# A fused two-layer cross-attention and expert kernel: new written-out orders for all five engines, and separate statistics tiles for the second row norm

## The chip, the core and the metric

The kernel runs on one core of one Trainium2 chip. A core has five engines with an instruction queue each: TensorE (PE, matrix products), ScalarE (ACT), VectorE (DVE), GpSimd (POOL) and SyncE (SP, which here only issues DMAs). They run side by side and meet at semaphores. The metric is the device time of one execution, in microseconds (us); less is better.

## What is computed

32 sequences of 128 rows by 128 features go through four steps, each added to its input. The letters a, b and c are the kernel's names for its stages.

```python
x = x + _L0_xattn_ref(_layernorm(x), ctx_1024, ctx_1024, mask_BxS2_if1, ...)   # a: 16 heads of 8, causal, bf16
x = x + _L0_ffn_ref(_layernorm(x), Ws1, Ws2, W1, W2, Wr)                       # a: shared part and 8 experts
x = x + _L1_xattn_ref(_layernorm(x), ctx_1024, mask_Bx1xSxS2_ff0, ...)         # b: 16 heads of 8, with a bias
x = x + _L1_ffn_ref(_layernorm(x), q_w, k_w, v_w, o_w, sel_v_w, sel_o_w, rs)   # c: 8 heads of 128, gated experts
...
def _L1_ffn_ref(x, q_w, k_w, v_w, o_w, sel_v_w, sel_o_w, route_scale):
    gate_v = _get_sel_gate(x, sel_v_w, rs)      # sigmoid, the best 2 of 8 experts for each head
    gate_o = _get_sel_gate(x, sel_o_w, rs)
    q = jnp.einsum('bsd,hpd->bhsp', x, q_w.reshape(H, P, D))
    k = jnp.einsum('bsd,hpd->bhsp', x, k_w.reshape(H, P, D))
    xv = jnp.einsum('bsd,hedp->bshep', x, v_w.reshape(H, E, D, P))
    v = jnp.einsum('bshep,bshe->bhsp', xv, gate_v)
    att = jax.nn.softmax(jnp.einsum('bhqp,bhkp->bhqk', q, k) * SCALE, axis=-1)
    ctx = jnp.einsum('bhqk,bhkp->bqhp', att, v)
    weighted = ctx[:, :, :, None, :] * gate_o[..., None]
    return jnp.einsum('bshep,hepd->bsd', weighted, o_w.reshape(H, E, P, D))
```

The last step is most of the work: all 64 value experts and all 64 output experts are computed for every row and weighted by gates that are zero for six of eight.

## The kernel before

**Stages.** Each batch (one sequence) passes four stages in a software pipeline of about five batches in flight. The calls beginning with `a_` are the first layer: the norm of x (`a_stats`, `a_root`, `a_norm`), the transposed context, keys and queries (`a_ctxt`, `a_keys`, `a_queries`), the scores and their maxima (`a_scores`, `a_max`, `a_maxt`, `a_withmax`), the second norm of the first layer (`a_stats2`, `a_root2`, `a_norm2`), its transpose `a_x1t`, and the experts. The `b_` calls are the second attention (`b_scores`, `b_bias` with the row maxima nmB, `b_exp`, `b_trans`, `b_proj`). The `c_` calls are the third norm (`c_stats`, `c_norm`, which writes xnC), its transpose `c_xt`, the routing (`c_choice`, `c_gates`), and the attention among rows (`c_products`, `c_scores`, `c_max`, `c_exp`, `c_trans`, `c_context`). `values(b, h)` and `outputs(b, h)` are the value and output experts of head h; on PE a third argument is the half of four experts.

**The experts on five engines.** For each half of four experts PE makes three products into one half of the PSUM tile psC (`Vh`, `Vl` or `Oh`, `Ol` are the two parts into which each weight is split). ACT multiplies the four blocks of one half by their gates into TE, DVE multiplies the four of the other half and adds what ACT has written, and POOL adds them up (`accO` for the outputs, `v_sb` for the values). psC has two halves that PE uses in turn, whatever it writes; scores and transposes of the `c_` part take turns in it too. The turn is kept by the helper `pair`:

```python
            def pair(key):
                p = place[key] = turn[0] % 2
                turn[0] += 1
                return psC[:, p], emptied[p]
```

so each write to a half waits for whoever reads it last.

**What sets the order.** Nothing is scheduled when the program is built. Each engine has three written-out lists of calls: `start()` (the fill), `period(i)`, called for i from 7 to 31 and unrolled, and `end()` (the drain). An engine does its list strictly in order, and every call waits at the semaphores of what it needs. A name may stand in another list in the changed file only because the place where the period is cut has been moved; what counts is the row of calls that results. SP's list holds the DMAs: `inputs(b)` (x and context), `masks`, `bias`, `b_keys` (12 small copies that build the block keys bdB), `a_keys` and `a_queries` (four small copies each, bdA and Qb), `store(b)`, and at the start the weights; `products2` loads `k_w`, `products` loads `q_w`. The 16 calls `load` and `cut` bring in and split the expert weights, beside the first two batches; ACT issues the loads.

**Row norms.** `spread` makes a norm's statistics in three operations on DVE, with POOL's `root` and DVE's `normal` behind it. The first and the second norm of a batch share stA, mvA and rsA.

## Time and profile before

| | us |
|---|---|
| median of 3 runs | 1480.84 (1480.16 to 1483.44) |
| the profiled execution | 1481.03 |
| its span | 1479.2 |
| fill (to the first `a_max` of batch 6) | 257.87 |
| 25 periods (to the first `a_max` of batch 31) | 1078.31 |
| drain | 143.02 |

| engine | busy, share of the span | busy in one part of a period, 815.47 to 834.37 | busy in the other, to 858.58 |
|---|---|---|---|
| PE | 95% | 18.60 of 18.90 | 24.14 of 24.21 |
| DVE | 87% | 17.06 | 22.10 |
| ACT | 86% | 18.90 | 20.05 |
| POOL | 58% | 10.41 | 16.18 |

A row of a timeline tells when an instruction (or several alike, with their count) started, how long it ran, and in brackets how long its engine had been idle before it and what ended that wait. The mean granted clock of TensorE was 0.979 of full, and it was full through the loop.

### The profile page before, as it was taken

To read this page: it belongs to the slowest core of one execution; us is meant where nothing else is said; L and a number is where in the kernel's file an instruction comes from. 1 tells how busy PE (TensorE), PEld (TensorE's weight loads), DVE (VectorE), ACT (ScalarE), POOL (GpSimd) and SP (SyncE) were. 2 spreads that over 40 slices of the span, in tenths; PEclk is the share of its full clock that TensorE was granted. 3 is DMA by queue.
4 is the path that set the end of the run, shared out by engine and by line. 5 is a ranking of instruction groups with operands and counts; after the bars stand their busy time and mean duration, and the time that the engine had idled before them with its cause. 6 is when DMAs were issued, how large, how long until landed. Compare 5 with 4: busy or idle time off the path is not lost.

```text
span 1479.2 us, 34876 instructions
## 1 busy us (share of the span) xinstructions
PE 1404.5 (95%) x9748; PEld 963.9 (65%) x9905; DVE 1283.9 (87%) x5266; ACT 1275.8 (86%) x4428; POOL 859.0 (58%) x1345
## 2 busy tenths in 40 slices
PE   4678999999999999999999999999999999999998
PEld 2455666666676666667666666766666676666654
DVE  3677988998998999899899999989999998998886
ACT  3657888899988889998888999888899988889886
POOL 3113656556565656656565565656556565655567
PEclk8689999999999999999999999999999999999999
DMA  4410000000000000000000000000000000000000
GB/s 136 139 56 16 10 14 16 15 15 12 15 11 14 16 15 15 12 15 11 14 16 15 15 13 15 11 14 16 15 15 13 15 11 14 14 15 7 8 3 4
DMA packets 68960, 30.18 MB, mean 20 GB/s; under 512 B 19168, under 2 KB 68768, under 8 KB 68768
## 3 DMA queue, kind: packets, MB, share of 16 engines
q1 hardware_dynamic: 51552, 19.31, 4.9%
q10 hardware_dynamic: 17216, 8.65, 2.1%
q8 instruction: 79, 1.29, 0.4%
q14 instruction: 113, 0.93, 0.2%
HBM read 17.31 MB, written 2.10 MB: 13 GB/s over the span
## 4 chain that ended last, share of the span: by engine, by line
PE 62%; ACT 13%; DVE 11%; POOL 7%; issue 4%; SPq 2%; DMA 1%; POOLq 0%; ACTq 0%; another core or an unknown queue 0%; DVEq 0%
PE psC L309 43%; PE psA L309 7%; PE psB L309 6%; DVE nmA L2240 5%; ACT PTA L1344 3%; ACT PS L1344 3%; POOL accO L3405 3%; DVE PTB L2365 3%; ACT TE L1344 3%; DVE TE L2497 2%; ACT PTB L1344 2%; SPq L3776 2%; PE psA L421 1%; POOL accO L3413 1%; PE psB L553 1%
## 5 line engine op out<-in xcount | busy, mean ns | idle before, releaser
L3405 POOL TENSOR_TENSOR accO<-accO,TE 128x512 f32<-128x512 f32 x192 | 246.3, 1283 | 143.9 <-DVE TE L2497 137.7
L1344 ACT ACTIVATE TE<-psC,gate 128x128 f32<-128x128 f32 x1024 | 300.1, 406 | 17.7 <-PE psC L309 10.4
L1344 ACT ACTIVATE TE<-psC,gateO 128x128 f32<-128x128 f32 x1024 | 292.5, 375 | 24.8 <-PE psC L309 16.2
L2497 DVE SCALAR_TENSOR_TENSOR TE<-psC,gate,TE 128x128 f32<-128x128 f32 x1024 | 284.5, 339 | 29.5 <-PE psC L309 18.4
L2497 DVE SCALAR_TENSOR_TENSOR TE<-psC,gateO,TE 128x128 f32<-128x128 f32 x1024 | 287.1, 341 | 13.2 <-PE psC L309 8.2
L3393 POOL TENSOR_TENSOR TE<-TE 128x256 f32<-128x256 f32 x256 | 192.4, 752 | 164.5 <-DVE TE L2497 160.4
L309 PE MATMUL psC<-Vh,xTh 128*128 128x512 f32 x512 | 263.3, 514 | 2.3 <-ACT PS L1344 1.2
L309 PE MATMUL psC<-Oh,ch 128*128 128x512 f32 x512 | 262.9, 513 | 0.2
L309 PE MATMUL psC<-Oh,cl 128*128 128x512 f32 x512 | 203.0, 396 | 0.0
L309 PE MATMUL psC<-Vh,xTl 128*128 128x512 f32 x512 | 202.5, 396 | 0.0
L309 PE MATMUL psC<-Ol,cb 128*128 128x512 bf16 x452 | 176.2, 390 | 0.0
L1344 ACT ACTIVATE PTB<-PTB,nmB 128x128 f32<-128x128 f32 x512 | 167.2, 434 | 3.5 <-DVE nmB L2365 3.5
L309 PE MATMUL psC<-Vl,xTb 128*128 128x512 bf16 x419 | 163.5, 390 | 0.0
L309 PEld LDWEIGHTS psC<-Ol,cb 128*128 128x128 bf16 x512 | 49.0, 96 | 140.6 <-issue 140.6
L309 PEld LDWEIGHTS psC<-Vl,xTb 128*128 128x128 bf16 x512 | 49.2, 96 | 139.5 <-issue 139.5
L3398 POOL TENSOR_TENSOR v_sb<-TE 128x128 f32<-128x128 f32 x256 | 118.5, 463 | 17.6
L2365 DVE CUSTOM_DVE_ANT_0 PTB<-psB,bias_sb 128x128 f32<-128x128 f32 x512 | 114.5, 284 | 3.2 <-PE psB L309 3.2
L309 PEld LDWEIGHTS psC<-Vh,xTh 128*128 128x128 f32 x512 | 98.7, 193 | 28.3 <-ACT PS L1344 10.5
L2240 DVE TENSOR_REDUCE nmA<-psA 128x4 f32<-128x512 f32 x128 | 84.8, 684 | 34.5 <-PE psA L309 34.3
L309 PEld LDWEIGHTS psC<-Oh,ch 128*128 128x128 f32 x512 | 99.0, 193 | 9.8 <-DVE cl L2489 0.9
L1344 ACT ACTIVATE PTA<-psA 128x512 f32<-128x512 f32 x160 | 101.7, 675 | 2.3 <-PE psA L309 1.2
L309 PEld LDWEIGHTS psC<-Oh,cl 128*128 128x128 f32 x512 | 97.6, 191 | 6.2
(228 smaller groups left out, 3426.7 us busy)
## 6 DMA issues: line engine op xcount, KB each, us to landing
bdB<-Kc SPq DMA_DIRECT2D x384, 16.0 KB
raw<-in_L_ffn_v_w ACTq DMA_DIRECT2D x8, 512.0 KB, 4.5
raw<-in_L_ffn_o_w ACTq DMA_DIRECT2D x8, 512.0 KB, 4.2
x_sb<-in_x SPq DMA_DIRECT2D x32, 64.0 KB, 2.1
ctx_sb<-in_ctx SPq DMA_DIRECT2D x32, 64.0 KB, 2.0
bdA<-Kc SPq DMA_DIRECT2D x128, 8.0 KB
Qb<-Qc SPq DMA_DIRECT2D x128, 8.0 KB
bias_sb<-in_mask_Bx1xSxS_ff SPq DMA_DIRECT2D x32, 64.0 KB, 1.9
```

The lines of the kernel that those rows point to most:

```text
L309: return T.matmul(o, l, r, start=start, stop=stop)
L421: m = T.transpose(psA[:, 1, t * P:(t + 1) * P], UA[:, t * P:(t + 1) * P], ident)
L553: m = T.transpose(psB[:, 1, t * P:(t + 1) * P], Qh1f[:, t * P:(t + 1) * P], ident)
L1344: return A.activation(o, i, func, **kw)
L2240: V.tensor_reduce(nmA[:, t, :], heads_of(psA[:, t % 2, :]), AX_X, ALU.max, negate=True).then_inc(a_nm, 1)
L2365: m = V.tensor_tensor_reduce(PTB[:, t, j], psB[:, t % 2, j * P:(j + 1) * P], bias_sb[:, b % 2], -1.0, LEAST, ALU.add, ALU.min, nmB[:, t, j ...
L2497: m = V.scalar_tensor_tensor(TE[:, i, e], psC[:, p, e * P:(e + 1) * P], gates[:, e:e + 1], TE[:, i, e], ALU.mult, ALU.add)
L3393: G.tensor_tensor(TE[:, i, 0:2], TE[:, i, 0:2], TE[:, i, 2:4], ALU.add).then_inc(v_fe, 1)
L3398: G.tensor_tensor(v_sb[:, h], TE[:, i, 0], TE[:, i, 1], ALU.add).then_inc(v_fe, 1)
L3405: G.tensor_tensor(accO[:], TE[:, slot(b, H1)] if h == 1 else accO[:], TE[:, slot(b, H1 + h)], ALU.add).then_inc(o_fe, 1)
L3413: G.tensor_tensor(accO[:, 0:2], accO[:, 0:2], accO[:, 2:4], ALU.add).then_inc(o_fe, 1)
L3776: SY.dma_start(dst, src).then_inc(s, 16)
```

## The change

**Statistics.** The second norm of the first layer gets tiles of its own, stA2, mvA2 and rsA2. **Order.** The lists of all five engines are written anew. Over the 32 batches each engine makes the same calls as before (2,562 on PE, 1,943 on ACT, 2,809 on DVE, 1,347 on POOL, 265 on SP), in another order.

```diff
         rsA = sb("rsA", [P, 1])
+        stA2 = sb("stA2", [P, 6])
+        mvA2 = sb("mvA2", [P, 2])
+        rsA2 = sb("rsA2", [P, 1])
...
-                spread(x1[:], stA, mvA, rsA, a_ln2, b, n)
+                spread(x1[:], stA2, mvA2, rsA2, a_ln2, b, n)
...
-                normal(xnA, x1[:], mvA, rsA, a_ln2)
+                normal(xnA, x1[:], mvA2, rsA2, a_ln2)
...
-                root(rsA, a_rs2)
+                root(rsA2, a_rs2)
...
+                a_x1t(i - 1)
+                b_proj(i - 2)
                 outputs(i - 4, 0, 1)
-                a_x1t(i - 1)
```

The places of the loop's and the fill's lists that matter most follow.

PE in a period, about the scores. `psC<-Oh,ch` and its two neighbours are one half of `outputs(i - 5, 7)`, `psB<-bdB,Qs` is `b_scores`, `psA<-bdA,Qb` with the mask's product is one `a_scores`, and `psC<-ident_r,xnC` is `c_xt`. Before:

```order
L309 MATMUL psC<-Oh,ch 128x512
L309 MATMUL psC<-Oh,cl 128x512
L309 MATMUL psC<-Ol,cb 128x512
L309 MATMUL psB<-bdB,Qs 128x512 x2
L309 MATMUL psA<-bdA,Qb 128x512
L309 MATMUL psA<-late_b,ident_b 128x4x44
L575 MATMUL psC<-ident_r,xnC 128x128
L309 MATMUL psA<-bdA,Qb 128x512
L309 MATMUL psA<-late_b,ident_b 128x4x44
L629 MATMUL psC<-ident_r,PS 128x128 x4
```

Now:

```order
L312 MATMUL psC<-Oh,ch 128x512
L312 MATMUL psC<-Oh,cl 128x512
L312 MATMUL psC<-Ol,cb 128x512
L312 MATMUL psA<-bdA,Qb 128x512
L312 MATMUL psA<-late_b,ident_b 128x4x44
L312 MATMUL psA<-bdA,Qb 128x512
L312 MATMUL psA<-late_b,ident_b 128x4x44
L578 MATMUL psC<-ident_r,xnC 128x128
L312 MATMUL psB<-bdB,Qs 128x512 x2
L632 MATMUL psC<-ident_r,PS 128x128 x4
```

Both first `a_scores` have moved ahead of the last two `b_scores`, and `c_xt` stands behind them.

DVE at the same place. `TE<-psC,gateO,TE` is `outputs(i - 5, 6)`, `nmA<-psA` is `a_max`, and the rows with nmB are `b_bias`. Before:

```order
L2365 ISA nmB 128x1
L2365 ISA PTB,nmB<-psB,bias_sb 128x128
L2365 ISA nmB 128x1
L2497 SCALAR_TENSOR_TENSOR TE<-psC,gateO,TE 128x128 x4
L2240 TENSOR_REDUCE nmA<-psA 128x4
L2365 ISA PTB,nmB<-psB,bias_sb 128x128
L2365 ISA nmB 128x1
L2365 ISA PTB,nmB<-psB,bias_sb 128x128
```

Now:

```order
L2368 ISA PTB,nmB<-psB,bias_sb 128x128
L2368 ISA nmB 128x1
L2500 SCALAR_TENSOR_TENSOR TE<-psC,gateO,TE 128x128 x4
L2223 TENSOR_SCALAR xnC<-x,mvC,rsC 128x128
L2243 TENSOR_REDUCE nmA<-psA 128x4
L2368 ISA PTB,nmB<-psB,bias_sb 128x128
L2368 ISA nmB 128x1
L2368 ISA PTB,nmB<-psB,bias_sb 128x128
L2368 ISA nmB 128x1
```

The third norm's last step (`xnC`, `c_norm`) stood 31 rows further ahead, and now stands between the outputs and the first `a_max`.

SP at the start of the fill. `in_L_ffn_q_w` and `in_L_ffn_k_w` are the weights of `products` and `products2`, and `in_x` with `in_ctx` is `inputs`. Before, from the 14th issue:

```order
L3776 DMA Ws2s<-in_L_ffn_Ws 64x128
L3776 DMA W2s<-in_L_ffn_W 128x4x128
L3776 DMA raw<-in_L_ffn_sel_v_w 64x128
L3776 DMA raw<-in_L_ffn_sel_o_w 64x128
L3776 DMA rs<-in_L_ffn_route_scale 128x1
L3776 DMA raw<-in_L_ffn_q_w 128x8x128
L3776 DMA mrow_i<-in_mask_BxS_if 16x128
L3776 DMA raw<-in_L_ffn_k_w 128x8x128
L3776 DMA bdA<-Kc 8x4x128 x4
L3776 DMA bdA<-keyrow 1x16x128
L3776 DMA Qb<-Qc 8x4x128 x4
L3776 DMA x_sb<-in_x 128x128
```

Now, from the 8th:

```order
L3779 DMA Wv1s<-in_L_xattn_wv 128x128
L3779 DMA Wo1s<-in_L_xattn_wo 128x128
L3779 DMA x_sb<-in_x 128x128
L3779 DMA ctx_sb<-in_ctx 128x128
L3787 DMA bq_raw<-in_L_xattn_bq 128x1x1
L3779 DMA raw<-in_L_ffn_k_w 128x8x128
L3779 DMA mrow_i<-in_mask_BxS_if 16x128
L3783 DMA bk_raw<-in_L_xattn_bk 128x1x1
L3779 DMA raw<-in_L_ffn_q_w 128x8x128
L3779 DMA x_sb<-in_x 128x128
L3779 DMA ctx_sb<-in_ctx 128x128
L3779 DMA Qb<-Qc 8x4x128 x4
```

The two large weights have moved ahead of the experts' weights of the first layer, and the inputs of batch 1 ahead of the block queries and keys.

On DVE `a_stats(i, 0)` of the next batch has moved from behind the values to right behind `a_maxt`, and in the fill `a_stats(1, 0)` stands ahead of the operations that build the block queries and keys of batch 0. In the drain DVE's `c_choice(31, 4)` and `c_choice(31, 5)`, which stood around `c_products(31, 0)`, stand behind `c_max(31, 1)`. On ACT, `c_xt` stands behind the copies of the keys in the fill where it stood ahead of them, and in a period `a_values2` and `values(1)` stand behind the last `a_exp`. On SP `bias(3)` stands ahead of `b_keys(2)`, where it stood between `b_keys(2)` and `a_keys(3)`.

## Rows read from the trace of the kernel before

**Rows 1.** The page: busy time and share of the span; granted clock, 40 slices.

```profile
PE 1404.5 (95%) x9748; PEld 963.9 (65%) x9905; DVE 1283.9 (87%) x5266; ACT 1275.8 (86%) x4428; POOL 859.0 (58%) x1345
...
PEclk8689999999999999999999999999999999999999
```

**Rows 2.** Busy time by stretch: fill, loop, a period's parts, half clock, drain.

```profile
core 0: us, PE busy (x) PEld busy (x) DVE busy (x) ACT busy (x) POOL busy (x), PEclk, DMA share, GB/s
0.00:257.87 257.87, 204.07 (x1400) 140.62 (x1420) 189.25 (x755) 185.08 (x601) 102.22 (x193) 0.89 0.20 56
257.87:1336.18 1078.31, 1069.06 (x7602) 739.09 (x7726) 978.44 (x4076) 973.98 (x3426) 665.27 (x1027) 1.00 0.05 14
815.47:834.37 18.90, 18.60 (x174) 13.24 (x175) 17.06 (x74) 18.90 (x68) 10.41 (x17) 1.00 0.06 15
834.37:858.58 24.21, 24.14 (x133) 16.32 (x135) 22.10 (x93) 20.05 (x72) 16.18 (x25) 1.00 0.06 14
24.90:65.90 41.00, 24.01 (x117) 15.36 (x117) 26.37 (x85) 24.81 (x61) 5.67 (x12) 0.50 0.54 150
1336.18:1479.20 143.02, 131.39 (x750) 84.20 (x761) 116.23 (x437) 116.77 (x403) 91.49 (x127) 0.99 0.02 5
```

**Rows 3.** ACT in one period: start, duration, line, operation, tiles, idle before.

```profile
815.47 1.14 ACT L1344 ACTIVATE TE<-psC,gateO 128x128 f32<-128x128 f32 x4 [0.30 <-PE psC L309]
...
818.68 0.29 ACT L1344 ACTIVATE xTh<-psC 128x128 fp32r<-128x128 f32 x1
```

**Rows 4.** Timeline of ACT, the same place one period later.

```profile
858.58 1.14 ACT L1344 ACTIVATE TE<-psC,gateO 128x128 f32<-128x128 f32 x4 [0.30 <-PE psC L309]
```

**Rows 5.** Waits in the loop: who waited for whom, total us, times, longest.

```profile
ACT ch L1344 <- PE psC L309: 32.1, 50, 0.7
...
PE psB L533 <- DVE nmB L2365: 4.8, 25, 0.2
```

**Rows 6.** Timeline of PE: the hand-over from ACT, and the scores.

```profile
834.37 0.50 PE L309 MATMUL psC<-Vh,xTh 128*128 128x512 f32 x1
...
817.40 0.82 PE L309 MATMUL psB<-bdB,Qs 128*128 128x512 f32 x2
818.07 0.39 PE L309 MATMUL psA<-bdA,Qb 128*128 128x512 bf16 x1
...
818.37 0.27 PE L575 MATMUL psC<-ident_r,xnC 128*128 128x128 f32 x1
```

**Rows 7.** Timeline of DVE at the same scores.

```profile
816.70 1.12 DVE L2497 SCALAR_TENSOR_TENSOR TE<-psC,gateO,TE 128x128 f32<-128x128 f32 x4
818.57 0.69 DVE L2240 TENSOR_REDUCE nmA<-psA 128x4 f32<-128x512 f32 x1 [0.76 <-PE psA L309]
```

**Rows 8.** Timelines in the fill: a row norm and the copy after it.

```profile
88.38 0.35 DVE L2220 TENSOR_SCALAR xnB<-x,mvB,rsB 128x128 f32<-128x128 f32 x1 [0.66 <-POOL rsB L3301]
...
89.17 0.28 ACT L1344 ACTIVATE xTB<-psB 128x128 f32<-128x128 f32 x1 [0.49 <-PE psB L500]
```

**Rows 9.** Issues of the block queries (SP), and PE waiting for them.

```profile
813.26 2.81 SPq L3776 DMA_DIRECT2D Qb<-Qc  x4
...
122.99 2.81 SPq L3776 DMA_DIRECT2D Qb<-Qc  x4
...
127.48 0.58 PE L309 MATMUL psA<-bdA,Qb 128*128 128x512 bf16 x1 [1.30 <-DMA Qb<-Qc]
```

**Rows 10.** First weights: issue (SP), product (PE), first cut (ACT).

```profile
0.80 0.71 SPq L3780 DMA_DIRECT2D bk_raw<-in_L_xattn_bk  x1
...
12.39 0.39 SPq L3776 DMA_DIRECT2D raw<-in_L_ffn_k_w  x1
...
17.24 3.78 PE L309 MATMUL psC<-raw 128*128 128x128 f32 x16 [4.88 <-DMA raw<-in_L_ffn_k_w]
...
25.13 1.15 ACT L1344 ACTIVATE Vh<-raw 128x512 fp32r<-128x512 f32 x2 [2.44 <-DMA raw<-in_L_ffn_v_w]
```

**Rows 11.** The drain: the longest wait of PE.

```profile
PE psC L309 <- ACT PS L1344: 1.2, 1, 1.2
```

More of the change, by code:

```diff
@@ L962, in start @@
                 outputs(1, 7, 1)
+                b_scores(4, 1)
+                outputs(1, 7, 0)
                 b_scores(4, 2)
-                outputs(1, 7, 0)
+                c_trans(2, 1)
+                c_xt(3)
                 b_scores(4, 3)
-                c_trans(2, 1)
                 a_scores(5, 0)
+                a_scores(5, 1)
                 b_trans(4, 0)
-                c_xt(3)
-                a_scores(5, 1)
+                values(2, 0, 1)
                 a_scores(5, 2)
-                values(2, 0, 1)
+                a_scores(5, 3)
+                b_trans(4, 1)
                 c_logits(3)
-                a_scores(5, 3)
                 c_products(3)
                 a_maxt(5)
-                b_trans(4, 1)
-                b_trans(4, 2)
                 values(2, 0, 0)
@@ L1746, in start @@
                 a_ctxt(3)
-                c_xt(1)
                 a_keys(3)
                 a_xt(3)
+                a_queries(3)
                 b_xt(2)
-                a_queries(3)
                 b_values(2)
+                c_xt(1)
+                a_values(3)
+                b_queries(2)
+                values(0, 0)
                 c_trans(0, 0)
                 c_trans(0, 1)
-                b_queries(2)
-                values(0, 0)
+                c_gexp(1)
+                a_values2(3)
                 b_exp(2, 0)
-                a_values(3)
-                c_gexp(1)
                 b_exp(2, 1)
@@ L2540, in start @@
                 cut(1)
+                a_stats(1, 1)
+                a_stats(1, 2)
                 a_attend(0, 0)
@@ L2608, in start @@
                 a_routed(1, 2)
-                c_stats(0, 2)
-                a_stats(2, 1)
+                cut(13)
                 a_stats(2, 2)
-                c_norm(0)
                 a_norm(2)
@@ L3929, in start @@
                 masks(5)
-                inputs(4)
-                bias(4)
                 a_masks(4)
+                inputs(5)
                 b_keys(3)
```

1256 lines of the change are left out of this document (628 added, 628 removed).

## The prediction, made before the changed kernel had run

> **What bounds the kernel now.** I read the page's busy times first [rows 1]: PE is at 95% of the span, DVE at 87%, ACT at 86%, and the granted clock is full outside the first stretches. Three engines stand this near to the whole span, so no average tells which of them sets the pace, and I split the span into stages [rows 2]. The fill runs to 257.87 us (where the first attention's maxima of batch 6 begin), the loop's 25 periods take 1078.31 us, 43.13 each, and the drain takes 143.02 us. The sum is 1479.20, and the profiled execution's time is 1481.03, 1.8 us around the span and 0.2 above the median of 1480.84.
>
> Then one period. ACT's copy of half `outputs(15, 6)` starts at 815.47 [rows 3] and the same copy of the next batch at 858.58 [rows 4]; both waited 0.30 for PE. Between them the period falls into two parts of different owners [rows 2]. From 815.47 to 834.37 ACT is busy for 18.90 of 18.90 us. At 834.37 PE takes up a half of psC that ACT's last exponentials of `c_exp` have read [rows 6], and from there to 858.58 PE is busy for 24.14 of 24.21 us. So a period is 18.90 us of ACT and 24.21 us of PE, with no gap worth naming in either. ACT's waits in the loop, the largest 32.1 us for `ch` [rows 5], lie in PE's part, where ACT has 4.16 us over, and cost nothing; PE's 4.8 us for `nmB` [rows 5] lie in ACT's part, and cost nothing either.
>
> **The change: the loop.** Written out over all 32 batches, each engine makes the same calls before and after: nothing is added, dropped or resized. What can move the time is only which call stands in which part, and what waits. I walked both parts through the new lists. ACT's part still holds the calls from `outputs(i, 6)` to the second `c_exp`, in another order (`a_values2` and `values(1)` later, `b_trans(3)` earlier), and PE's part still holds everything from `values(3, 1)` to `outputs(6, 1)`. Nothing crosses. If nothing waits, the parts are 18.90 and 24.21 as before, and the term is 25 x 0 = 0. From below it is bounded by PE's 0.07 us of idle in its part: 25 x 0.07 = 1.8 us at most, unless a call crosses after all. From above it is bounded by the two new waits that I find tight.
>
> The first is the third row norm, `c_norm`. It stood early among the outputs; now it stands behind DVE's `outputs(6)`, right ahead of `a_max(0)`. DVE's four adds start at 816.70 and take 1.12 [rows 7], so the norm can start at about 817.75. In the fill an equal norm at 88.38 led to ACT's copy at 89.17, 0.79 us later [rows 8], so ACT can have `xTh` at 818.54. It takes it at 818.68 now [rows 3]: 0.14 us in hand, no cost if all else holds. DVE pays nothing for the norm there, since it waited 0.76 for PE at `a_max(0)` [rows 7].
>
> The second is that PE makes `a_scores(0)` and `a_scores(1)` ahead of the last two `b_scores`, so it wants the block queries Qb at 817.40 instead of 818.07 [rows 6]. SP's four issues end at 813.26 + 2.81 = 816.07. In batch 3 of the fill they ended at 125.80 and PE, which waited, ran at 127.48, 1.68 later [rows 9]; by that row Qb would be there at 817.75, and PE would stand 0.35. The loop's queues are emptier than the fill's, and `a_queries` comes one place earlier on PE, so I take 0 for it, and keep 0.35 less the hand that ACT has for the range. It matters only because `c_xt` is queued behind these scores on PE, and ACT's `xTh` behind that: two scores of 0.30 us (818.07 to 818.37 [rows 6] is one with its mask), then the transpose and the copy, 817.75 + 0.60 + 0.79 - 0.35 (the norm's own time) = 818.79, 0.11 late.
>
> The other moves of the loop have cover. The early `a_stats` is a first operation of the next batch's norm, three short instructions on DVE in ACT's part, where DVE is busy for 17.06 of 18.90 us [rows 2]; it is what the second set of statistics tiles allows, since with one set `a_stats(i+1)` would overwrite the statistics that `a_norm2(i)` still reads. Moving `a_x1t` and `b_proj` ahead of `outputs(0, 1)` leaves PE's work in its part alone. SP's `inputs` and `store` wait on things that come once in a period, and nothing urgent is queued behind them.
>
> **The change: the fill.** Here the order matters most, since in 257.87 us PE is busy for only 204.07, partly at half clock [rows 2]. SP's first issue is at 0.80, and the query weights `q_w` are its 19th and the key weights `k_w` its 21st, at 12.39; PE waited 4.88 us for them, made the product at 17.24 in 3.78 us, and the first cut of the expert weights began on ACT at 25.13 after 2.44 us of waiting for its load [rows 10]. In the new list `k_w` is the 13th and `q_w` the 16th issue. One issue takes (12.39 - 0.80) / 20 = 0.58 us in the mean, a wait within them included, which puts the last of the pair at 0.80 + 15 x 0.58 = 9.5, or near 9.0 without that wait. The product comes 2.9 to 3.4 us sooner, and the load chain of the 16 cuts with it. Against it: DVE's first statistics of batch 1 now stand ahead of the work that builds the block queries and keys, and wait for inputs that SP issues as its 17th and 18th, so the first scores of batch 0 come 2 to 2.5 us later. Batches 0 and 1 are paced by both chains in turn; I take them as cancelling, -0.5 after batch 1, with -2 and +1 as ends. For batches 2 and 3, `bias(3)` leaves the run of SP issues that PE waits on (one issue of 0.44 us; PE waited 1.30 there [rows 9]), and ACT's three copies of `c_xt` leave the place ahead of the key copy, 0.5 us: together some -1.5. In batches 4 and 5 the norms leave the place ahead of `b_queries`; I take -1, from 0 to -2. The fill's sum is -0.5 - 1.5 - 1 = -3.0, and its ends are -6 and +1.5 with the uncertain cancellation.
>
> **The change: the drain.** PE is busy for 131.39 of 143.02 us [rows 2], but its longest single wait is 1.2 us, for the exponentials PS [rows 11], and the rest of its idle time is behind the last products, where POOL's sums are the end of the kernel and keep their order. DVE's `c_choice(31, 4)` and `(31, 5)` leave the place ahead of the maxima that this wait hangs on; they are two of the short selections, so I take -0.5 of the 1.2, with -1.2 and 0 as ends.
>
> **Sum.** 0 - 3.0 - 0.5 = -3.5 us: 1481.03 - 3.5 = 1477.5 against the profiled execution, and 1480.84 - 3.5 = 1477.3 against the median, which I forecast.
>
> **A rule on the clock.** From 24.90 to 65.90 us the granted clock is 0.50, PE at 1.2 GHz, with PE busy for 24.01 of 41.00 us; before it fell PE had stood idle for long stretches, 4.88 us of them ahead of the product [rows 2, 10]. At 2.4 GHz those 24.01 us would be 12.0. The Trainium skill, TensorE: Matmul & The Clock Gate, section "What's actually happening", states that throttled is the default and that activity releases it. By that rule a fill whose PE works without long gaps would run faster than my terms say, by up to 12 us; by mine, which leave the gaps where loads and other engines put them, by nothing. ACT is busy for 24.81 of the same 41.00 us, so I don't expect the gaps to close.
>
> **The rivals.**
>
> Slower: the scores and the row norm arrive late. The mechanism is ACT's `xTh`, which stands in the part where ACT has no gap, so each period pays in full. Price: from 0.11 us (the late Qb) to 0.76 - 0.14 = 0.62 us (the norm late by all of the wait that DVE has there), times 25: +2.8 to +15.5. It decides from 0.14 us of delay at 818.54. In the middle, 0.3 us a period, it gives 1477.3 + 7.5 = 1484.8. For it: two fresh dependencies with 0.14 us of cover. Against: DVE's adds ahead of the norm have their times from rows, and DVE is free there. Chance 0.25, of which 0.22 slower than the bound.
>
> Faster in the loop: the hand-over between the two parts moves. If a call of ACT's part comes to lie in PE's part, where ACT has 4.16 us over, the period shrinks by that call's time; one short copy is about 0.3 us [rows 3], 25 x 0.3 = 7.5, giving 1469.8. For it: ACT starts its part after a wait of 0.30 for PE, which another order could shift. Against: the calls on both sides of the hand-overs are the same. Chance 0.15.
>
> Faster in the fill: the clock is granted sooner there. Up to -12 as above, about -5 with ACT nearly as busy: 1472.3. Chance 0.08.
>
> Nothing: the product comes sooner, but the head's later scores of batch 0 are carried through to the loop, and the drain's wait turns into another. Sum between -1 and +1, 1480.8. Chance 0.10.
>
> **How the numbers follow.** The forecast keeps 0.42. A measurement of this kernel tells about 0.2%, 3 us, from no change, so "faster" begins at 1477.9. The forecast's own spread (1474 to 1480) straddles that: 0.27 of it is faster, 0.15 the same. Faster: 0.27 + 0.15 + 0.08 = 0.50. Same: 0.15 + 0.10 + 0.03 of the slow rival's low end = 0.28. Slower: 0.22. The range takes in most of both sides' rivals: from 1465, between the loop's -7.5 and the two gains together, to 1487, above the slow rival's middle.
>
> **What would show it.** The starts of ACT's copy of `outputs(i, 6)` should still be 43.1 us apart in the changed kernel; 0.1 more, with a wait at `xTh` for PE, is the slow rival, and less means that a call has crossed. ACT should be busy for all of its part and PE for all of its own. The product of `q_w` and `k_w` should start near 14, the first cut near 22, and the first scores later than now. The maxima of batch 6 should begin near 255 instead of 257.87, and the drain should take about 142.5 us with PE's wait for PS shorter. What would make the forecast wrong outright is a delay on ACT's part that I took to be covered, since everything there is multiplied by 25, or a fill whose chains I cancelled and which don't.

## The result: 31 us slower, most of it in the loop

The changed kernel takes 1512.93 us in the median of 4 runs (1512.5 to 1513.3), the kernel before 1481.5 in 4 runs beside it (1480.16 to 1483.44). The ratio is 1.0211, with a 95% interval from 1.0193 to 1.0229. The forecast was 1477.3 and its range ended at 1487, so the time is outside it, on the side of the rival that I called slower.

**The page of after**, busy times and granted clock, as [rows 1]:

```profile
PE 1420.7 (94%) x9749; PEld 958.9 (63%) x9905; DVE 1354.8 (90%) x5266; ACT 1288.4 (85%) x4428; POOL 857.4 (57%) x1345
...
PEclk9989999999999999999999999999999999999999
```

The calls are the same and their number is the same, yet DVE is busy for 70.9 us more (1354.8 against 1283.9). POOL is busy for 1.6 us less. That is the line to stop at: instructions of DVE have become longer.

**The same stretches of after**, as [rows 2]: fill, loop, the two parts of a period, and from ACT's second context copy of batch 31 to the end. The columns are those of [rows 2].

```profile
core 0: us, PE busy (x) PEld busy (x) DVE busy (x) ACT busy (x) POOL busy (x), PEclk, DMA share, GB/s
0.00:262.54 262.54, 206.85 (x1399) 139.45 (x1417) 199.99 (x754) 185.89 (x601) 102.09 (x194) 0.97 0.20 55
262.54:1365.12 1102.58, 1080.70 (x7606) 736.00 (x7732) 1033.43 (x4085) 985.84 (x3430) 663.91 (x1026) 1.00 0.05 14
832.90:852.45 19.55, 18.71 (x173) 13.24 (x174) 18.66 (x77) 19.00 (x68) 11.82 (x19) 1.00 0.03 7
852.45:877.04 24.59, 24.52 (x133) 16.17 (x135) 22.74 (x89) 20.40 (x72) 14.74 (x23) 1.00 0.07 20
1353.87:1510.30 156.43, 144.33 (x805) 90.70 (x819) 131.88 (x483) 126.51 (x437) 100.87 (x139) 0.99 0.02 5
```

ACT's part of a period went from 18.90 to 19.55 us and PE's part from 24.21 to 24.59, a period from 43.11 to 44.14. In ACT's part ACT now has 0.55 us of idle time where it had none; DVE is busy for 18.66 there, where it was for 17.06. ACT makes 68 and 72 instructions in the two parts and PE 173 and 133, as before (174 and 133), so each part still has the owner that it had, and each owner now waits for something.

Where the 31.1 us of the span come from is told best by one mark that both kernels have, the ACT copy `ctxTb` of a batch. It comes 2.9 us later in batch 4, 5.9 later in batch 8 (339.91 against 334.04) and 27.8 later in batch 31 (1353.87 against 1326.11). So the way to batch 8 costs 5.9, the 23 periods from batch 8 to batch 31 cost 21.9, 0.95 each, and the rest, the drain, costs 3.3. By the prediction's own marks (the first maxima of batches 6 and 31) it is 4.7 for the fill, 24.3 for the loop and 2.1 for the drain.

**What ACT and PE wait for.** After, the loop: who waited for whom, total us, times, longest.

```profile
PE psC L578 <- DVE xnC L2223: 14.6, 24, 0.7
...
ACT xTh L1347 <- PE psC L578: 12.5, 24, 0.6
...
PEld psC L312 <- DVE TE L2500: 7.8, 46, 0.2
```

None of the three stands among the waits of before's loop. The first two are one chain: DVE's norm xnC is late, so PE's `c_xt` is, and so is ACT's `xTh`, in the part in which ACT has no gap. That is the place that the prediction named. Its reason was not the one that the prediction named.

**Why xnC is late.** A core keeps its tiles in two memories, SBUF and PSUM (psA, psB and psC lie in PSUM, the others in SBUF). The four adds read PSUM; the norm reads and writes SBUF alone. One period of after on DVE, POOL, PE and ACT, in this order.

```profile
834.14 1.12 DVE L2500 SCALAR_TENSOR_TENSOR TE<-psC,gateO,TE 128x128 f32<-128x128 f32 x4
835.18 1.17 DVE L2223 TENSOR_SCALAR xnC<-x,mvC,rsC 128x128 f32<-128x128 f32 x1
836.27 0.68 DVE L2243 TENSOR_REDUCE nmA<-psA 128x4 f32<-128x512 f32 x1
```

```profile
835.00 2.69 POOL L3408 TENSOR_TENSOR accO<-accO,TE 128x512 f32<-128x512 f32 x2
```

```profile
836.41 0.33 PE L578 MATMUL psC<-ident_r,xnC 128*128 128x128 f32 x1 [0.63 <-DVE xnC L2223]
```

```profile
836.77 0.28 ACT L1347 ACTIVATE xTh<-psC 128x128 fp32r<-128x128 f32 x1 [0.55 <-PE psC L578]
```

The norm has no idle time ahead of it and starts when the four adds end, as I said it would. But it takes 1.17 us, where an equal norm took 0.35 in [rows 8]. POOL's two sums started at 835.00 and take 1.34 each; the first of them is over at about 836.3, and the norm at 836.35. The norm sits in its own duration until POOL is through with an instruction that it had begun. In all 18 batches from 8 to 25 of after the norm begins while POOL runs; in before it did so in none of them. The durations of all 32 norms, before and then after (ns, least/median/most):

```profile
engine op xcount: duration ns min/median/max, first and last start us, forms
L2220 DVE TENSOR_SCALAR xnC<-x,mvC,rsC x32: 260/338/1371, 85.2 to 1411.2; 128x128 f32<-128x128 f32 x32
```

```profile
L2223 DVE TENSOR_SCALAR xnC<-x,mvC,rsC x32: 334/1172/1294, 82.9 to 1442.7; 128x128 f32<-128x128 f32 x32
```

The trace of before had one norm of 1371 ns among its 32, and POOL's sum had started at the same 164.03 as that norm, so this was to be seen before the run, in the extremes and not in one typical row.

The Trainium skill, SBUF — State Buffer, section "Who interferes with whom", states that DVE's second pair of SBUF ports is GpSimd's too, that whoever issues first has it for the whole instruction, and that the other is blocked; that `tensor_scalar` is among the operations that can take the pair, when their operands meet its conditions, and that an instruction with two SBUF inputs contends with GpSimd's reads. The rows above agree with it for a DVE instruction that comes second, the norm's 1.17 us and its end 0.08 us behind POOL's above all. They don't show the other direction: a sum of POOL that began 0.16 us behind a DVE instruction (838.88, below) took 0.73 us, as long as one that began first. Which ports the norm takes isn't seen in a trace, only that it waits.

**The second place.** PE's part, on DVE and POOL, in after. `ob` and the sum x are `a_first`.

```profile
856.70 0.21 DVE L2282 TENSOR_TENSOR ob<-obA,bob 128x128 bf16<-128x128 bf16 x1
856.95 0.79 DVE L2285 TENSOR_TENSOR x<-x_sb,ob 128x128 f32<-128x128 f32 x1
857.67 1.11 DVE L2500 SCALAR_TENSOR_TENSOR TE<-psC,gate,TE 128x128 f32<-128x128 f32 x4
```

```profile
856.87 0.73 POOL L3396 TENSOR_TENSOR TE<-TE 128x256 f32<-128x256 f32 x1 [0.24 <-DVE TE L2500]
```

And the same sum before:

```profile
838.72 0.28 DVE L2282 TENSOR_TENSOR x<-x_sb,ob 128x128 f32<-128x128 f32 x1
```

```profile
838.88 0.73 POOL L3393 TENSOR_TENSOR TE<-TE 128x256 f32<-128x256 f32 x1
```

POOL's sum of the values is released by DVE's own four adds. In before x stood right behind the adds and began 0.16 us ahead of POOL. In after the short `ob` stands between, x begins 0.08 us behind POOL and takes 0.79 instead of 0.28. The next norm, xnA, and the selection gp<-first,gp meet later sums: their medians go from 336 to 751 and from 274 to 720 ns. The values' adds behind them are late, and PE's weight loads wait for TE. POOL's own end is not what is waited for: in the loop of after no engine has a wait of 0.15 us or more that POOL ends.

### The profile page after: what moved, and what is told of

It reads as the page before. It is cut to its first block, busy times and chain, and to the rows that moved or that the text cites. A ratio compares the mean times of both kernels' runs of the same rounds, so it can differ in the third digit from the quotient of the medians.

```text
span 1510.3 us, 34857 instructions
## 1 busy us (share of the span) xinstructions
PE 1420.7 (94%) x9749; PEld 958.9 (63%) x9905; DVE 1354.8 (90%) x5266; ACT 1288.4 (85%) x4428; POOL 857.4 (57%) x1345
## 3 DMA queue, kind: packets, MB, share of 16 engines
q8 instruction: 79, 1.29, 0.4%
## 4 chain that ended last, share of the span: by engine, by line
PE 48%; ACT 22%; DVE 10%; issue 4%; POOL 3%; SPq 1%; DMA 0%; POOLq 0%; another core or an unknown queue 0%; ACTq 0%; DVEq 0%
PE psC L312 35%; ACT PTB L1347 8%; PE psA L312 5%; DVE TE L2500 5%; ACT TE L1347 4%; ACT PTA L1347 3%; PE psB L312 3%; ACT PS L1347 2%; DVE PTB L2368 2%; DVE xnC L2223 2%; ACT yh L1347 1%; PE psA L424 1%; POOL accO L3408 1%; POOL TE L3396 1%; PE psB L556 1%
## 5 line engine op out<-in xcount | busy, mean ns | idle before, releaser
L3396 POOL TENSOR_TENSOR TE<-TE 128x256 f32<-128x256 f32 x256 | 186.9, 730 | 149.4 <-DVE TE L2500 147.0
L312 PE MATMUL psC<-Ol,cb 128*128 128x512 bf16 x475 | 185.4, 390 | 0.0
L312 PEld LDWEIGHTS psC<-Vh,xTh 128*128 128x128 f32 x512 | 98.6, 193 | 38.1 <-ACT PTC L1347 10.5
L312 PEld LDWEIGHTS psC<-Vh,xTl 128*128 128x128 f32 x512 | 97.5, 190 | 5.8 <-issue 0.2
L1347 ACT ACTIVATE PTA<-psA 128x512 f32<-128x512 f32 x160 | 91.7, 635 | 10.3 <-PE psA L312 8.7
```

What stands on the lines that cost most here:

```text
L312: return T.matmul(o, l, r, start=start, stop=stop)
L1347: return A.activation(o, i, func, **kw)
L3396: G.tensor_tensor(TE[:, i, 0:2], TE[:, i, 0:2], TE[:, i, 2:4], ALU.add).then_inc(v_fe, 1)
```

## The experiments

**P** is the theory of the port: a DVE instruction whose operands lie in SBUF alone, and that starts while POOL runs, waits inside its duration. Its rival **O** is that of the prediction: the place of the norm in DVE's list makes it late, whatever POOL does. Where calls are moved, the lists were written out flat for all batches, and one batch stands for all. A period is the typical distance of the same ACT copy from batch to batch in the steady loop, 43.12 in before and 44.13 in after; single batches take up to 0.8 longer (0.16 in before), so a mean over all lies up to 0.1 above. Kernels here whose loop has the order of before read from 43.10 to 43.17, so a difference under 0.07 says nothing. Each ratio is to the kernel before, run beside the changed one (medians 1482.2 to 1482.9).

### The norm put back, and the norm alone moved

In after, DVE's list (b from 6 to 27):

```diff
 outputs(b - 2, 1)
+c_norm(b)
...
 outputs(b - 2, 6)
-c_norm(b)
 a_max(b + 2, 0)
```

> The changed kernel with one call moved back on VectorE: for batches 6 to 27, c_norm(b) stands behind outputs(b-2, 1) again instead of behind outputs(b-2, 6). Theory P (a VectorE instruction that reads and writes SBUF only can't run while GpSimd runs one, and waits inside its own duration): xnC was 1.11 us in the changed kernel because it starts 0.18 us after a 1.29 us add of accO; back at its old place it is near 0.34 us, ScalarE's wait at xTh (0.50 a period) goes, and the period falls from 44.13 by 0.6 to 0.7 to about 43.5; what is left above 43.12 is the same effect at other instructions (x, xnA). Rival O (the new place of the norm is late by itself, without any stretching): the same period gain, but the instruction's duration would be 0.34 in both kernels, which the changed kernel's trace already speaks against; it expects 43.5 too. Rival S (scores and block queries are late, not the norm): period stays at 44.1.

Measured: 1498.56 us, ratio to before 1.0105 (1.0076 to 1.0134), period 43.47. The norm has a median of 336 ns again. That gives back 0.66 of the 1.01 us a period and leaves 0.35; x, xnA and gp are as long as in after (0.79, 0.75, 0.72).

In before, the same move the other way (b from 6 to 27):

```diff
 outputs(b - 2, 1)
-c_norm(b)
...
 outputs(b - 2, 6)
+c_norm(b)
 a_max(b + 2, 0)
```

> The kernel before with the one call moved the other way on VectorE: for batches 6 to 27, c_norm(b) stands behind outputs(b-2, 6). Theory P: what the late norm costs depends on what GpSimd runs at that moment. In the old order GpSimd has its sum for head 5 done by then, so xnC can be short (0.34 us) and the period stays within 0.15 us of 43.12; if GpSimd's sum for head 6 gets in first, xnC is over 1 us and the period is 43.6 to 43.8. Rival O: the place alone costs, so the period rises to 43.6 or more with xnC at 0.34 us.

Measured: 1481.51 us, 0.9992 (0.998 to 1.0004), period 43.11. DVE and then POOL:

```profile
819.04 0.34 DVE L5566 TENSOR_SCALAR xnC<-x,mvC,rsC 128x128 f32<-128x128 f32 x1
```

```profile
819.21 1.31 POOL L8832 TENSOR_TENSOR accO<-accO,TE 128x512 f32<-128x512 f32 x1 [1.33 <-DVE TE L5843]
```

This is the first experiment that parts the two theories. The norm stands between the same neighbours as in after, behind the adds and ahead of `a_max(0)`, and costs nothing, because POOL had been idle for 1.33 us and its sum starts 0.17 us after the norm. O expected a period of 43.6 or more. The place on DVE is half of the cause; POOL's list should be the other half, and the next two experiments change POOL alone.

### Making POOL's work short, and putting it back

In after, the sums of heads 5 and 6 on POOL work on 16 of 512 columns, so that POOL starts at the same moments and soon ends (the kernel leaves most of these two heads out of its result):

```diff
+if h in (5, 6):
+    G.tensor_tensor(accO[:, 0, 0:16], accO[:, 0, 0:16], TE[:, slot(b, H1 + h), 0, 0:16],
+                    ALU.add).then_inc(o_fe, 1)
+    return
```

> The changed kernel in its own order, with one size changed: GpSimd's sums for heads 5 and 6 of the output experts work on 16 of 512 columns (so these heads are left out of the result). Nothing on VectorE, ScalarE, TensorE or SyncE is changed. Theory P: with no long GpSimd instruction under it, xnC falls from 1.11 to about 0.35 us where it stands, the wait at xTh goes and the period falls by 0.5 to 0.7, to 43.4 to 43.6. Rival O: xnC's place is late whatever GpSimd does, and the period stays at 44.1 within 0.1.

Measured: 1497.24 us, 1.0094 (1.0068 to 1.0119), period 43.46. DVE and POOL:

```profile
828.30 0.33 DVE L5569 TENSOR_SCALAR xnC<-x,mvC,rsC 128x128 f32<-128x128 f32 x1
```

```profile
828.12 0.59 POOL L8836 TENSOR_TENSOR accO<-accO,TE 128x16 f32<-128x16 f32 x2
```

All 18 norms of batches 8 to 25 still start while POOL's sum runs, 0.04 to 0.06 us ahead of its end, and take only 0.34. What costs is POOL's remaining duration and not the overlap as such, nor any order on DVE, which is that of after to the last call.

In after, POOL's list (b from 8 to 23): the sum of head 5 ahead of the selections, where before had it.

```diff
 outputs(b, 4)
+outputs(b, 5)
 c_gates(b + 1, 0)
 c_gates(b + 1, 1)
 c_gates(b + 1, 2)
-outputs(b, 5)
 outputs(b, 6)
```

> The changed kernel with one move on GpSimd: for batches 8 to 23 (16 periods), outputs(b, 5) stands ahead of the three c_gates(b+1) instead of behind them. All work is kept. The add then starts about 1.3 us sooner and is over when VectorE comes to xnC. Theory P: in these 16 periods xnC is near 0.35 us and the period is 43.4 to 43.6, in the others 44.13; the total falls by about 16 x 0.6 = 10 us, to about 1503. Rival O: no change, 1513.

Measured: 1501.34 us, 1.0124 (1.0094 to 1.0153). The 16 periods with the move take 43.47 (one takes 44.27), the others 44.13. All work is kept here. The norms of these periods take 0.48, since they start 0.01 us behind a selection of POOL that takes 0.40; the 0.14 more than 0.34 cost nothing, as much as the prediction had in hand. So three different edits (the norm back, the sums short, the sum's place back) each give the same 43.46 or 43.47: they undo one and the same thing.

### The rest of the loop

On top of the first experiment, POOL's first value sum on 16 of 128 columns in each block, from batch 1 (most of that sum is left out of the result):

```diff
-    G.tensor_tensor(TE[:, i, 0:2], TE[:, i, 0:2], TE[:, i, 2:4], ALU.add).then_inc(v_fe, 1)
+    w = 16 if b else P
+    G.tensor_tensor(TE[:, i, 0:2, 0:w], TE[:, i, 0:2, 0:w], TE[:, i, 2:4, 0:w], ALU.add).then_inc(v_fe, 1)
```

> e1_norm_back with one size changed: GpSimd's first sum of the value experts (TE<-TE) works on 16 of 128 columns of each block from batch 1 on, so most of that sum is left out of the result. VectorE's order is untouched. Theory P: e1's period of 43.47 is still 0.35 above the old one because x (0.79 us), xnA (0.75) and gp (0.72) wait for these sums; with the sums short, x and gp fall to about 0.3 and the period to 43.1 to 43.2. Rival O2 (the new order in TensorE's part costs 0.35 by itself, by a_x1t or the norms standing earlier): the period stays at 43.4 to 43.5.

Measured: 1487.29 us, 1.0028 (1.0014 to 1.0043), period 43.18. x takes 0.31 and gp 0.29, and the norm of the first layer is short again:

```profile
L5569 DVE TENSOR_SCALAR xnA<-x,mvA,rsA x32: 336/345/829, 41.5 to 1364.8; 128x128 f32<-128x128 f32 x32
```

With both collisions out, 0.95 of the 1.01 us a period are gone while all of the new order stands but one call. So P explains the loop: 0.66 us at xnC and 0.29 at x, xnA and gp; the 0.06 left are within the spread of one order. The 0.66 is shown with all of POOL's work kept. The 0.29 is shown only with most of a sum left out: what speaks against a mere relief of POOL is that no engine in the loop waits 0.15 us or more for POOL's end.

Also on top of the first, the call `a_first(b, 0)` on DVE, which makes `ob`, ahead of `values(b - 3, 4)` as in before (b from 11 to 30), to have x directly behind the adds:

```diff
 values(b - 3, 3)
-values(b - 3, 4)
 a_first(b, 0)
+values(b - 3, 4)
 a_first(b, 1)
```

> e1_norm_back with one more call moved back on VectorE: for batches 11 to 30 a_first(b, 0) stands ahead of values(b-3, 4) again, so that a_first(b, 1), which reads x_sb and ob and writes x, comes directly behind VectorE's add for that head instead of behind a short instruction. Theory P with the detail that the first to start wins: x starts before GpSimd's sum that this add releases, and falls from 0.79 to 0.28 us; xnA may still wait. The period falls from 43.47 by 0.1 to 0.35. Rival O2: x is short or not, the period stays.

Measured: 1508.12 us, 1.0172 (1.0142 to 1.0201), period 43.88. x is down to 0.28, as P says, but the period grew by 0.41. DVE's largest wait in it:

```profile
DVE ob L5628 <- ACT obA L3260: 19.4, 19, 1.0
```

A call moved back alone meets neighbours that are not back. In the new order PE and ACT make what `ob` reads later, so DVE stands for 1.0 us ahead of the adds on which PE waits. This expectation was wrong for the time: this one call takes out the collision of x, but not without a larger wait.

### Both halves put into before

If both halves are needed, both together in before should make it slower. In before, the norm late as above, and on POOL (b from 8 to 23):

```diff
 outputs(b, 4)
-outputs(b, 5)
 c_gates(b + 1, 0)
 c_gates(b + 1, 1)
 c_gates(b + 1, 2)
+outputs(b, 5)
 outputs(b, 6)
```

> The kernel before with two moves that do nothing alone: c_norm(b) behind outputs(b-2, 6) on VectorE (as in e2, period 43.11) and, on GpSimd, for batches 8 to 23 the three c_gates(b+1) between outputs(b, 4) and outputs(b, 5), as the changed kernel has them. Theory P: the gates put GpSimd's 1.29 us sum for head 5 under the norm, so in these 16 periods xnC takes about 1.1 us and the period is 43.5 to 43.8, elsewhere 43.11; the whole is 6 to 11 us above the kernel before. Rival O: as in e2 no loss, 43.11 throughout.

Measured: 1482.8 us, 0.9995 (0.9984 to 1.0006), period 43.11; a miss. The sum of head 5 ran from 816.37 to 817.65, 0.65 us ahead of the norm at 818.30. In before POOL has so much room here that the selections don't push its sum far enough. Two more calls were needed on POOL (same batches):

```diff
 c_gates(b + 1, 2)
-outputs(b, 5)
-outputs(b, 6)
 a_values(b + 4)
 a_masks(b + 5)
+outputs(b, 5)
+outputs(b, 6)
 outputs(b, 7)
```

> e11 missed: its GpSimd finished the sum for head 5 0.64 us before the norm, so the norm started first. Here, in the same kernel (order of before, norm late), GpSimd also makes a_values and a_masks ahead of the sum for head 5, for batches 8 to 23: 1.06 us more, so the sum should start at about 0.9 us before the norm and end 0.4 us after the norm's start. Theory P (whoever starts first holds the other up): xnC takes 0.7 to 0.9 us in these 16 periods, the copy xTh is 0.2 to 0.5 us late and the period is 43.3 to 43.6; everywhere else 43.11. Rival O: 43.11 throughout, since the norm's own place was shown to cost nothing.

Measured: 1485.52 us, 1.002 (1.0009 to 1.0031). The 16 periods with the move take 43.30, the others 43.12. POOL, then DVE, then all norms:

```profile
818.51 2.71 POOL L8832 TENSOR_TENSOR accO<-accO,TE 128x512 f32<-128x512 f32 x2
```

```profile
819.20 0.70 DVE L5566 TENSOR_SCALAR xnC<-x,mvC,rsC 128x128 f32<-128x128 f32 x1
```

```profile
L5566 DVE TENSOR_SCALAR xnC<-x,mvC,rsC x32: 258/690/1385, 84.6 to 1414.5; 128x128 f32<-128x128 f32 x32
```

The sum starts 0.69 us ahead of the norm and its first instruction (1.29 long) has some 0.61 left; the norm takes 0.70. The period pays 0.18 of the norm's 0.36, since 0.14 were in hand. So, with the norm late, the effect is made in before as well by POOL's list alone, and its size follows what POOL has left. All the norms xnC that a POOL sum or selection holds up, in all the kernels here, tell the same: they end about 0.08 us behind POOL's instruction, so they take what it has left and 0.08 more, and never less than 0.34 (left 0.39: 0.48, in the fourth experiment; 0.61: 0.70, here; 1.09: 1.17, in after). POOL's instruction on one column is an exception: `root` had 0.48 us left at the norm of batch 1 of after, and that norm took 0.35. Beside it, the statistics tiles alone, in before:

```diff
-                spread(x1[:], stA, mvA, rsA, a_ln2, b, n)
+                spread(x1[:], stA2, mvA2, rsA2, a_ln2, b, n)
```

> The kernel before with the separate statistics tiles alone and every order unchanged. All theories: no change, within 0.1% of the kernel before and a period of 43.1.

Measured: 1483.38 us, 1.0003 (0.9992 to 1.0014). The tiles cost and give nothing of themselves.

### The fill

The first product of the weights, the first scores and the first maxima of after, on PE, SP and DVE, beside [rows 10]:

```profile
14.06 3.78 PE L312 MATMUL psC<-raw 128*128 128x128 f32 x16 [2.87 <-DMA raw<-in_L_ffn_q_w]
...
24.52 0.59 PE L312 MATMUL psA<-bdA,Qb 128*128 128x512 bf16 x1 [6.67 <-DMA bdA<-keyrow]
```

```profile
15.65 3.08 SPq L3779 DMA_DIRECT2D Qb<-Qc  x4
...
21.69 0.57 SPq L3779 DMA_DIRECT2D bdA<-keyrow  x1
```

```profile
25.29 1.29 DVE L2243 TENSOR_REDUCE nmA<-psA 128x4 f32<-128x512 f32 x2 [7.53 <-PE psA L312]
```

The product starts at 14.06, as forecast, and the first cut at 21.84. But the first maxima come at 25.29 instead of 21.69, 3.6 later, since the block copies are issued later (`keyrow` at 21.69, before at 16.14). ACT's list has calls that hang on these maxima between the cuts, so the second cut is at 31.96 where it was at 28.51, and the 3.3 us gained are lost by the second of 16. Two theories: **H**, the head's own order (statistics of batch 1 first on DVE, inputs first on SP) makes it late; **D**, the large loads of the expert weights, now in flight earlier, hold the small copies up.

In after, H undone:

```diff
 keys0()                  # DVE
-a_stats(1, 0)
 columns()
...
 operand_k()
+a_stats(1, 0)
 a_max(0, 0)
...
 loads1()                 # SP
+keys0()
 inputs(0)
 queries0()
 products2()
 masks(0)
-keys0()
```

> The changed kernel with two moves at the head of the fill: on VectorE a_stats(1, 0) stands behind operand_k, and on SyncE the load of the key bias stands ahead of the inputs of batch 0. Theory H: the first scores' maxima start at 25.3 instead of 21.7 because VectorE waited 2.5 us for the key bias and 1.9 us for batch 1's inputs ahead of the work that builds the block keys and queries, and all batches of the fill stay behind by that: the maxima start at 21.5 to 23, and the whole is 2 to 3 us shorter than 1512.9. Rival L (the loads of the expert weights pace the fill, so the head does not matter): the maxima come sooner, the whole stays within 1 us.

Measured: 1513.95 us, 1.0211 (1.0182 to 1.0241), first maxima at 24.95. A miss: `keyrow` is issued 1.65 sooner, at 20.04, and lands only at 24.09, so PE starts at 24.18.

In before, the large weights ahead on SP as in after:

```diff
 loads1()
-weights_ffn()
 weights_switch()
 products()
 masks(0)
 products2()
+weights_ffn()
 a_keys(0)
```

> The kernel before with one move on SyncE: the five loads of the first layer's expert weights (weights_ffn) stand behind those of the query and key weights. My prediction's term: the product of the two comes about 2.5 us sooner, the cuts of the expert weights with it. If the load chain paces the fill, the whole is 1 to 3 us shorter than the kernel before; if the first layer's attention paces it (theory H), it is the same within 0.7 us.

Measured: 1488.04 us, 1.0038 (1.0022 to 1.0054). The product comes at 15.14, 2.1 sooner, and the kernel is 6 us slower, which neither side of the expectation allowed. SP and PE:

```profile
18.52 2.84 SPq L10204 DMA_DIRECT2D Qb<-Qc  x4
```

```profile
25.44 0.59 PE L309 MATMUL psA<-bdA,Qb 128*128 128x512 bf16 x1 [6.92 <-issue]
```

The last of the four small copies of Qb is issued at 20.68 and lands at 25.24, 4.56 us later; the two expert loads of 512 KB each had been issued by ACT at 18.56 and 19.04. The first maxima are at 26.21. To see whether the loads do it, ACT's first load was made to wait for the first scores, on top of that:

```diff
 act.wait_ge(s_M, 1)
-load(0)
 copy(flat(M[:]), psC[:, 0, :], scale=SCALE1).then_inc(s_Mdone, 1)
+act.wait_ge(a_s, 1)
+load(0)
```

> e8_weights_first with one wait moved: ScalarE issues the first two loads of expert weights (512 KB each) only after TensorE has begun the first scores, instead of right after the product of the query and key weights. Theory D (the early product lets the expert loads start earlier, and the small copies that build the block queries and keys then share the DMA engines with them and land late): in e8 the block queries landed 4.6 us after their last issue at 20.7 against 1.8 in the kernel before; here they land at about 22.5, the first maxima start at 23.2 to 23.6 instead of 26.2. Rival (the small copies are late because of where SyncE issues them alone): the maxima stay at 26.2. Of the whole I expect 0 to 3 us less than e8's 1488.0, since the cuts lose what the scores gain.

Measured: 1484.85 us, 1.0015 (1.0004 to 1.0026). The last issue of Qb at 21.13 landed at 22.94, 1.8 us later, and the maxima are at 23.66. D holds: the loads cost the small copies 2.8 us. The other 1.8 of the 4.5 us by which the maxima were late is their later issue (the last at 20.68, in before at 18.92), which this experiment left as it was.

The same wait in after, first without H undone:

```diff
-load(0)
 copy(flat(M[:]), psC[:, 0, :], scale=SCALE1).then_inc(s_Mdone, 1)
+act.wait_ge(a_s, 1)
+load(0)
```

> The changed kernel with the same wait: ScalarE issues the first expert loads only after the first scores have begun. By theory D the last of the block operands, issued at 21.7 to 22.3, lands 1.8 us later, so the first maxima start at about 24.3 instead of 25.3, and the whole stays within 2 us of 1512.9, because the cuts start later. By the rival nothing changes before the first scores.

Measured: 1513.36 us, 1.0201 (1.0171 to 1.023), first maxima at 24.71, `keyrow` issued at 22.12. By itself it moves the maxima by 0.6 us, H did by 0.3, and neither moves the whole. Then both edits together in after:

```diff
-a_stats(1, 0)            # DVE, now behind operand_k()
...
+keys0()                  # SP, now ahead of inputs(0)
...
+act.wait_ge(a_s, 1)      # ACT, ahead of load(0)
```

> e7_head and e10_loads_wait_after in one kernel: the head's moves and the expert loads held back until the first scores. Each alone moved the first maxima by 0.3 and 0.6 us of the 3.6. In e7 the last small copy was issued 1.65 us sooner and TensorE still had it only at 24.18, because the expert loads were in flight; in e10 nothing was in flight, but it was issued late, at 22.12. Theory D+H (two causes, each enough): both together put the last issue near 20.4 and its landing near 22, so the first maxima start at 22.5 to 23.1, about 2.5 us sooner than in the changed kernel. If a third cause holds them, they stay above 24. The whole: 0 to 2.5 us less than 1512.9, since e10's held-back loads had given nothing.

Measured: 1511.65 us, 1.0196 (1.0166 to 1.0225). PE:

```profile
21.85 0.59 PE L312 MATMUL psA<-bdA,Qb 128*128 128x512 bf16 x1 [4.12 <-DMA bdA<-keyrow]
```

The maxima come at 22.62, 2.7 sooner. Each of the two causes is enough to hold the first scores up, so either alone shows little when it is taken out. ACT's `xTh` of batch 8 is 2.6 us earlier than in after (437.06 against 439.64), that of batch 26 1.8 (1232.03 against 1233.87), and the end 1.1 by span and 1.3 by the medians. So the gain of the head shrinks through the loop and the drain, in a period of 44.17 where after has 44.13. That difference is no larger than between runs of one order, and the kernel was run twice, so whether the head's gain reaches the end is not shown.

### Fill and drain by themselves

The order of after up to `outputs(4, 0)` of each engine's list, and that of before from there. A piece of SP's list, as one of many places:

```diff
 masks(5)
-inputs(4)
-bias(4)
 a_masks(4)
+inputs(5)
 b_keys(3)
```

> Each engine follows the changed kernel's order up to its first call of outputs(4, 0), and from there the order of the kernel before for all that is left. It prices the new fill alone. From the marks of the two full kernels (first maxima 3.6 us later, still 3.9 at batch 5) I expect the loop at 43.1 and the whole 3 to 5 us above the kernel before. Rival: the old loop gives the delay back as its first periods catch up, within 1 us.

Measured: 1489.77 us, 1.0042 (1.0022 to 1.0062). The mark is 6.5 us later in batch 8 and 6.6 in batch 31, the loop has its 43.1. I expected 3 to 5; the new fill costs 6 to 7, of which 2.9 are there by batch 4.

The order of before up to `outputs(26, 0)`, and that of after from there. A piece of DVE's list:

```diff
-c_choice(31, 4)
 c_products(31, 0)
-c_choice(31, 5)
...
 c_max(31, 1)
+c_choice(31, 4)
+c_choice(31, 5)
 c_choice(31, 6)
```

> Each engine follows the order of the kernel before up to its first call of outputs(26, 0), and from there the changed kernel's order for what is left. It prices the new drain, with some four of the last periods. From the marks of the full kernels, 4 x 1.0 for those periods at most and about 1 to 2 us for the drain: 2 to 5 us above the kernel before. My prediction said 0.5 us below it.

Measured: 1487.38 us, 1.0032 (1.002 to 1.0043): 1.6 us up to batch 31 and 3.4 behind it, where after has 3.3. DVE is busy for 132.26 us behind the mark, before for 125.05. Two of its groups there (with shapes, count, busy time and mean ns):

```profile
L5569 DVE TENSOR_SCALAR xnC<-x,mvC,rsC 128x128 f32<-128x128 f32 x3 | 2.2, 727 | 0.2 <-POOL rsC L8731 0.2
...
L5602 DVE TENSOR_TENSOR MtA<-nmA,MtA 128x16 bf16<-128x16 f32 x1 | 1.3, 1287 | 0.0
```

MtA took 0.22 in before. Of the 7.2 us more, most stand in groups of this kind, operands in SBUF alone (one more norm falls behind the mark, 0.3 of it), and PE's weight load waits 0.7 us for MtA. That fits P; no run took the collision out of the drain, so for the drain it is argued and not shown.

## Why the prediction was wrong, step by step

**"Nothing crosses. If nothing waits, the parts are 18.90 and 24.21."** Right as far as it went. No call crossed, and with the collisions out the period was 43.18.

**"The norm can start at about 817.75 ... so ACT can have `xTh` at 818.54 ... 0.14 us in hand."** This is the step that failed. The start was right: the norm stood right behind the adds. The 0.79 us from the norm's start to the copy came from a row of the fill in which POOL did nothing. Its duration was taken as the instruction's own, and it is not: it depends on what POOL is doing when it starts. In after the copy came 836.77 - 835.18 = 1.59 after the norm's start, 0.80 more than I took, and the longer norm accounts for it: 1.17 against the row's 0.35. Less the 0.14 in hand, 0.80 is the 0.66 us a period that three experiments gave back. The term of the sum that this step made 25 x 0 = 0 measured 24.3 us. The moves on POOL's list, which decided it, were read as "the same calls in another order" and costed at nothing. The rows of before even show how narrow it was: the adds end at 817.8, and POOL's next sum started at 817.89. In before the norm would have won by a tenth of a microsecond, and the second experiment shows that it does, by 0.17.

**The rival "Slower" had the right place, and a bound that was too low.** It named ACT's `xTh`, a full payment in each period, and 0.11 to 0.62 us. Measured for this place: 0.66. Its mechanism (late by DVE's wait ahead of the norm, or by Qb) was wrong: DVE has no wait there, and PE's wait is for xnC and not for Qb. Neither did it have the second place.

**"The other moves of the loop have cover."** Wrong by 0.29 us a period. `ob` between the adds and x is what gave POOL the first move. I had looked at which engine has time over, and DVE's own part of PE's stretch has 2.11 us over [rows 2]; but PE waits there for single adds, not for DVE's sum of work. What cover the early `a_stats` had was not taken apart.

**The fill, -3.0 with ends -6 and +1.5.** It was +4.7 by the prediction's mark, and +5.9 up to batch 8. The term "product 2.9 to 3.4 us sooner" was right (3.2) and worth nothing, since the cut after next hangs on the first maxima. "The first scores of batch 0 come 2 to 2.5 us later" was mis-sized: 3.6, because earlier weights also put the expert loads in front of the small copies. And "I take them as cancelling" was the wrong choice of form: the later of two chains sets the time, so a gain on one and a loss on the other don't add up to nothing. The terms for batches 2 to 5, together -2.5, did not come: the mark lost 2.9 by batch 4 and 5.9 by batch 8. With both causes of the late head taken out, batch 4 is only 0.3 us later than in before (159.35 against 159.04), so the head accounts for the first 3 us. Of the second 3 us, between batch 4 and batch 8, two thirds go with the loop's collisions, already at work: before takes 175.00 us for them and after 177.98, DVE is busy for 10.5 us more there, and x takes 0.7 to 0.8 us from batch 4 on, where it took 0.29 up to batch 3. The kernel with POOL's value sums short takes 175.97, 1.8 less than the same kernel with them whole (177.73), and the norm put back had given 0.25. The last 1.0 was not separated.

**The drain, -0.5.** It was +2.1 by the prediction's mark, and +3.3 behind ACT's copy of batch 31. PE's wait for PS is still 1.2 to 1.4 us. The step looked at one wait and not at what the moved operations meet.

**The clock.** The rival of a sooner granted clock did not come about: in after the product of `W1s` has the same mean of 1131 ns near 30 to 60 us as in before, against a median of 676 ns over all batches in both, so that stretch ran at the same low level, 1.2 GHz.

## What to carry to other kernels

Where VectorE and GpSimd both work near the bound, a reorder of one list is a change of the other's durations: for each moved VectorE instruction whose operands lie in SBUF alone, look up what GpSimd is doing at its new start, and allow for it what GpSimd's instruction has left (here that made 0.34 us into 1.17, 25 times). Look at the longest duration of an instruction in the trace and not at a typical row: one of 32 at four times the median is the price of a collision that the order has so far avoided. Put such an instruction directly behind the one that releases GpSimd, with nothing short between, or where GpSimd waits for something else.

## What was not expected of the hardware

- A norm of 128x128 in fp32 takes 0.34 us alone and 1.17 behind a sum of GpSimd just begun, with no idle time ahead of it and no row among DVE's waits: only its duration tells. It ends 0.08 us behind GpSimd's instruction. Two 128x128 inputs in SBUF: 0.28 and 0.79.
- A DVE instruction that starts first isn't held up, and one that starts second is, by as little as 0.08 us (POOL at 856.87, x at 856.95, 0.79 long) or, the other way, by 0.16 (x at 838.72, 0.28 long, POOL at 838.88).
- Four copies of 8 KB landed 1.8 us after their last issue with no expert load in flight, and 4.56 us after it behind two loads of 512 KB from another engine's queue.
- The mean granted clock of the fill reads 0.97 in after and 0.89 in before, while the same products between 30 and 60 us take 1131 ns in both: for 24.90 to 65.90 us the profile says 0.50 in before and 1.00 in after. A granted clock of 1.00 in a stretch is to be held against the duration of a product before it is believed.
